# A two-pass graph layer with a gated feed-forward layer: table scatters spread over more groups, and four steps moved at the opening of both passes

## The reference, cut to what matters

```python
# x [50000, 256]; src, dst [50000]; 50000 edges
x = x + gnn(layernorm(x)); x = x + ffn(layernorm(x))
gnn(x) = x @ W1.T + b1 + (segment_sum(x[dst], src) / max(count, 1)) @ W2.T + b2
ffn(x) = shared_mlp(x) + sum over the top 2 of 4 experts of gate * expert_mlp(x)
```

## Time and profile before

| | us |
|---|---|
| median of 3 runs | 3266.72 (3265.14 to 3267.07) |
| profiled execution | 3267.08 |
| its span, from first to last instruction | 3265.5 |
| busy PE, DVE, ACT, POOL | 3104.3, 2673.0, 1944.1, 1831.9 |

### The profile page before, as it was taken

One profiled execution on the slowest core, in us unless ns is written; L12 is line 12 of the kernel. 1 busy time (PEld: TensorE's weight loads), 2 busy tenths in 40 slices (PEclk: granted clock), 3 DMA queues, 4 the chain that ended last, 5 costly groups with the idle time before them and its releaser, 6 DMA issues.

```text
span 3265.5 us, 61478 instructions
## 1 busy us (share of the span) xinstructions
PE 3104.3 (95%) x20817; PEld 2846.7 (87%) x20817; DVE 2673.0 (82%) x7212; ACT 1944.1 (60%) x3507; POOL 1831.9 (56%) x1554
## 2 busy tenths in 40 slices
PE   6988889989949999999999999999999999999998
PEld 6988888889948888888888888888888888888987
DVE  7878878786438888888888888888888888888886
ACT  4655555555626656566665656666665656666565
POOL 1688888888445554555555555555555555555540
PEclk9998899999979999999999999999999999999999
DMA  8776666676643333333333333333333333333330
GB/s 247 205 186 180 178 195 180 177 198 179 180 126 89 97 93 89 98 84 99 85 100 92 91 97 84 97 83 101 90 94 98 85 98 84 99 87 97 93 82 26
DMA packets 201856, 387.38 MB, mean 119 GB/s; under 512 B 106703, under 2 KB 109853, under 8 KB 201538
## 3 DMA queue, kind: packets, MB, share of 16 engines
q1 hardware_dynamic: 133938, 226.03, 25.6%
q10 hardware_dynamic: 30800, 102.42, 9.8%
q0 software_dynamic: 36800, 54.95, 7.2%
HBM read 236.11 MB, written 161.00 MB: 122 GB/s over the span
## 4 chain that ended last, share of the span: by engine, by line
PE 70%; DVE 0%; ACT 0%; DMA 0%; POOL 0%; issue 0%; SPq 0%; POOLq 0%; DVEq 0%
PE acc L1129 25%; PE acc L1190 13%; PE acc L1099 12%; PE acc L1110 4%; PE acc L1112 4%; PE acc L1176 3%; PE acc L1153 3%; PE acc L1186 1%; PE acc L1145 1%; PE acc L1201 1%; PE acc L1139 1%; DMA tab<-tab_d 0%; POOL e_oh L178 0%; POOL rows L166 0%; ACT h2f L1234 0%
## 5 line engine op out<-in xcount | busy, mean ns | idle before, releaser
L166 POOL DMA_INDIRECT rows<-z_d,tab x500 | 568.1, 1136 | 645.2 <-DMA tab<-tab_d 486.0
L178 POOL TENSOR_SCALAR e_oh<-iota_sb,tab 128x250 fp32r<-128x250 f32 (+1 forms) x500 | 522.6, 1056 | 470.2 <-PE acc L1112 466.5
L1129 PE MATMUL acc<-x1T_hi,wl_hl 128*128 128x500 f32 x2400 | 665.4, 392 | 0.0
L387 POOL DMA_INDIRECT tab_d<-pair,idx x400 | 555.0, 1387 | 118.9 <-issue 104.7
L726 PE MATMUL acc<-w_hl,xT_hi 128*125 128x256 f32 x3200 | 586.6, 289 | 0.0
L1129 PEld LDWEIGHTS acc<-x1T_hi,wl_hl 128*128 128x128 f32 x2400 | 444.0, 188 | 84.0
L726 PEld LDWEIGHTS acc<-w_hl,xT_hi 128*125 128x125 f32 x3200 | 483.2, 195 | 0.0
L1190 PE MATMUL acc<-wl_hl,h_hi 128*125 128x256 f32 x2400 | 477.7, 281 | 0.0
L1391 DVE TENSOR_TENSOR h_lo<-h1f,h_hi 128x500 fp32r<-128x500 f32 x600 | 396.8, 674 | 49.1 <-ACT h_hi L1228 39.7
L1221 ACT ACTIVATE h1f<-acc,bl_sb 128x500 f32<-128x500 f32 x600 | 404.2, 674 | 14.4
L1190 PEld LDWEIGHTS acc<-wl_hl,h_hi 128*125 128x125 f32 x2400 | 390.6, 185 | 3.7
(11 more groups left out here) (145 smaller groups left out, 6400.8 us busy)
## 6 DMA issues: line engine op xcount, KB each, us to landing
xs<-in_x SPq DMA_DIRECT2D x100, 448.0 KB
z_d<-zs ACTq DMA_DIRECT2D x100, 448.0 KB
y_d<-ys ACTq DMA_DIRECT2D x100, 448.0 KB
y_sb<-y_d SPq DMA_DIRECT2D x100, 448.0 KB
x_sb<-in_x SPq DMA_DIRECT2D x100, 448.0 KB
out<-x_sb SPq DMA_DIRECT2D x100, 448.0 KB
codes_b<-code_d SPq DMA_DIRECT2D x25, 390.6 KB
rows<-z_d,tab POOLq DMA_INDIRECT x500
```

Of the source, the lines that this page charges most:

```text
L166: pool.indirect_dma_start(out=rows[g.h][:, q, :], out_offset=None, in_=z_d, in_offset=bass.IndirectOffsetOnAxis(ap=tab[g.h][:, q, 0:1], ax ...
L178: pool.tensor_scalar(e_oh[:, q, w], iota_sb[:, w], tab[g.h][:, q, 1:2].bitcast(F32), None, ALU.is_equal).then_inc(S["e_oh_ready"], 1)
L387: pool.indirect_dma_start(out=tab_d, out_offset=bass.IndirectOffsetOnAxis(ap=idx[:, n:n + 1], axis=0), in_=pair[:, 2 * n:2 * n + ROW], in_ ...
L1129: mm = pe.matmul(bank[L1_BANKS[t]][:, 0:GN], wl1_hl[:, w, f, t * P:(t + 1) * P], (x1T_hi, x1T_lo)[a][:, f, :], start=n == 0, stop=n == 5)
```

## The change

The 400 scatters are spread over groups 8 to 96 with 9 for two groups, where 5 a group were done by group 87; three come before the power of an even group instead of two. The low bias row goes to partition 32 and is written there by DVE; `two_ones` is all ones (the other rows of `bias_r` are zero). SP's head loses the fills, which are issued two a group for groups 0 to 4, and the weights and constants of the main pass, which follow at groups 20 and 24; targets come before the identity. DVE takes the statistics and negative bias of groups 0 and 1 earlier, PE the edge transposes before group 0's. In the main pass, at step -2 alone, POOL's gathers come after the power.

```diff
@@ -57,7 +57,6 @@
 OB = 4
 G_WTS = 84
 NSC = 8
-PER_G = 5
 WINDOW = ((0, 2), (0, 2), (0, NS), (2, NS), (2, NS))
 
 
@@ -206,7 +205,6 @@
                 st_b = sb("st_b", [1, 2, D], F32, c0)
                 st_bs = sb("st_bs", [1, D], F32, c0)
                 st_bh = sb("st_bh", [1, D], F32R, c0)
-                st_bl = sb("st_bl", [1, D], F32R, c0)
                 b3_hi = sb("b3_hi", [NB3, D], F32R, c0)
                 b3_lo = sb("b3_lo", [NB3, D], F32, c0)
 
@@ -252,7 +250,6 @@
                 s_flo = sem("ffn_weights_low")
                 s_small = sem("small_weight_step")
                 s_bs = sem("bias_ready")
-                s_row = sem("bias_row_moved")
                 s_fillset = sem("fill_set")
                 s_filled = sem("table_filled")
                 s_one = sem("ones_ready")
@@ -313,14 +310,14 @@
                               .then_inc(s_bc[m % 2], 16)
 
                         sp.dma_start(ei[:, 0], src).then_inc(s_src, 16)
-                        sp.dma_start(code2[:], codes).then_inc(s_c2, 16)
                         load_x(0)
                         load_x(1)
                         sp.dma_start(st_w12[:, :, 0:D], w1t).then_inc(s_w12, 16)
                         sp.dma_start(st_w12[:, :, D:2 * D], w2t).then_inc(s_w12, 16)
                         sp.dma_start(st_b[:], b12.partition_broadcast(1)).then_inc(s_w12, 16)
+                        sp.dma_start(ei[:, 1], dst).then_inc(s_dst, 16)
                         sp.dma_start(ident_sb[:], ident).then_inc(s_id, 16)
-                        sp.dma_start(ei[:, 1], dst).then_inc(s_dst, 16)
+                        sp.dma_start(code2[:], codes).then_inc(s_c2, 16)
                         load_x(2)
                         load_x(3)
                         sp.wait_ge(s_code, 1)
@@ -330,27 +327,29 @@
                         sp.wait_ge(s_codest, 16)
                         load_codes(0)
                         load_codes(1)
-                        sp.wait_ge(s_fillset, 3)
-                        for k in range(NFILL):
-                            sp.dma_start(fill_v[0][:, k * FILL:(k + 1) * FILL], fill[:])\
-                              .then_inc(s_filled, 16)
-                        sp.wait_ge(s_bs, 7)
-                        sp.dma_start(bias_r[1:2].bitcast(F32), st_bl[:].bitcast(F32)).then_inc(s_row, 16)
-                        sp.dma_start(st_wl1[:], wl1).then_inc(s_wl, 16)
-                        sp.dma_start(st_wl2[:], wl2).then_inc(s_wl, 16)
-                        sp.dma_start(st_wl3[:], wl3).then_inc(s_wl, 16)
-                        sp.dma_start(st_gw[:], gw).then_inc(s_wl, 16)
-                        sp.dma_start(st_b3[:], b3).then_inc(s_wl, 16)
-                        sp.dma_start(st_sel[:], selg).then_inc(s_wl, 16)
-                        sp.dma_start(iota_sb[:], iota).then_inc(s_cst, 16)
-                        sp.dma_start(bl1_sb[:], bl1).then_inc(s_cst, 16)
-                        sp.dma_start(bl2_sb[:], bl2).then_inc(s_cst, 16)
-                        sp.dma_start(gb_sb[:], gb.partition_broadcast(P)).then_inc(s_cst, 16)
-                        sp.dma_start(tie_sb[:], tie).then_inc(s_cst, 16)
                         blocks = 2
                         for g in range(NG):
                             if g + XB < NG:
                                 load_x(g + XB)
+                            if g == 0:
+                                sp.wait_ge(s_fillset, 3)
+                            if 2 * g < NFILL:
+                                for k in (2 * g, 2 * g + 1):
+                                    sp.dma_start(fill_v[0][:, k * FILL:(k + 1) * FILL], fill[:])\
+                                      .then_inc(s_filled, 16)
+                            if g == 20:
+                                sp.dma_start(st_wl1[:], wl1).then_inc(s_wl, 16)
+                                sp.dma_start(st_wl2[:], wl2).then_inc(s_wl, 16)
+                                sp.dma_start(st_wl3[:], wl3).then_inc(s_wl, 16)
+                            if g == 24:
+                                sp.dma_start(st_gw[:], gw).then_inc(s_wl, 16)
+                                sp.dma_start(st_b3[:], b3).then_inc(s_wl, 16)
+                                sp.dma_start(st_sel[:], selg).then_inc(s_wl, 16)
+                                sp.dma_start(iota_sb[:], iota).then_inc(s_cst, 16)
+                                sp.dma_start(bl1_sb[:], bl1).then_inc(s_cst, 16)
+                                sp.dma_start(bl2_sb[:], bl2).then_inc(s_cst, 16)
+                                sp.dma_start(gb_sb[:], gb.partition_broadcast(P)).then_inc(s_cst, 16)
+                                sp.dma_start(tie_sb[:], tie).then_inc(s_cst, 16)
                             if blocks < NCH // CB4 and CB4 * (blocks - 1) <= last_chunk(g) + 1:
                                 load_codes(blocks)
                                 blocks += 1
@@ -394,13 +393,14 @@
                         rstd(1)
                         for g in range(NG):
                             if g >= G_SCAT:
-                                n = (g - G_SCAT) * PER_G
-                                for e in range(n, min(n + 2, EC)):
+                                n = min(EC, (g - G_SCAT) * 9 // 2)
+                                m = min(EC, (g + 1 - G_SCAT) * 9 // 2)
+                                for e in range(n, min(n + 3, m)):
                                     scatter(e)
                             if g % 2 == 0 and g + 4 < NG:
                                 rstd(g // 2 + 2)
                             if g >= G_SCAT:
-                                for e in range(n + 2, min(n + PER_G, EC)):
+                                for e in range(n + 3, m):
                                     scatter(e)
                         for h in range(NSC):
                             pool.wait_ge(s_scat[h], 16 * (EC // NSC))
@@ -546,7 +546,7 @@
                         dve.memset(ones16[:], 1.0).then_inc(s_one, 1)
                         dve.memset(zeros16[:], 0.0).then_inc(s_one, 1)
                         dve.memset(bias_r[:].bitcast(F32), 0.0).then_inc(s_bs, 1)
-                        dve.memset(two_ones[:].bitcast(F32), 0.0).then_inc(s_bs, 1)
+                        dve.memset(two_ones[:].bitcast(F32), 1.0).then_inc(s_bs, 1)
                         dve.memset(half_neg[:], -0.5).then_inc(s_bs, 1)
                         dve.memset(fill[:], 0).then_inc(s_fillset, 1)
                         dve.memset(pair[:], 0).then_inc(s_fillset, 1)
@@ -567,6 +567,7 @@
                         dve.wait_ge(s_half, 1)
                         dve.scalar_tensor_tensor(out=code16[:], in0=c_g, scalar=2.0, in1=c_h,
                                                  op0=ALU.mult, op1=ALU.add).then_inc(s_code, 1)
+                        stats(0)
                         dve.wait_ge(s_dst, 16)
                         dve.tensor_copy(flat[:, 0], ei[:, 1]).then_inc(s_flat, 1)
                         step(dve.tensor_scalar(c_t, c_s[:], float(SP_), 1.0, ALU.mult, ALU.add))
@@ -575,22 +576,19 @@
                         dve.scalar_tensor_tensor(out=flat[:, 2], in0=c_h, scalar=float(HALF),
                                                  in1=c_l, op0=ALU.mult,
                                                  op1=ALU.add).then_inc(s_flat, 1)
+                        neg_bias(0)
                         dve.wait_ge(s_w12, 16 * 3)
                         dve.tensor_tensor(st_bs[:], st_b[:, 0], st_b[:, 1], ALU.add).then_inc(s_bs, 1)
                         dve.wait_ge(s_bs, 4)
-                        dve.memset(two_ones[0:2].bitcast(F32), 1.0).then_inc(s_bs, 1)
                         dve.tensor_copy(st_bh[:], st_bs[:]).then_inc(s_bs, 1)
-                        dve.wait_ge(s_bs, 6)
-                        dve.tensor_tensor(st_bl[:], st_bs[:], st_bh[:].bitcast(F32),
+                        dve.wait_ge(s_bs, 5)
+                        dve.tensor_tensor(bias_r[32:33], st_bs[:], st_bh[:].bitcast(F32),
                                           ALU.subtract).then_inc(s_bs, 1)
                         dve.tensor_copy(bias_r[0:1], st_bh[:].bitcast(F32)).then_inc(s_bs, 1)
                         dve.wait_ge(s_whi, 1)
                         dve.tensor_tensor(w12_hl[:, 1], st_w12[:], w12_hl[:, 0].bitcast(F32),
                                           ALU.subtract).then_inc(s_wlo, 1)
-                        stats(0)
-                        neg_bias(0)
                         stats(1)
-                        neg_bias(1)
                         low(0)
                         for a in range(2):
                             dve.wait_ge(s_tr, a + 1)
@@ -600,6 +598,7 @@
                                 dve.tensor_copy(to[:, :, :, 0], got).then_inc(s_ev, 1)
                             else:
                                 dve.tensor_copy(to[:, :, :, 1].bitcast(F32), got).then_inc(s_ev, 1)
+                        neg_bias(1)
                         dve.wait_ge(s_c2, 16)
 
```

(9 more changed lines are left out.)

## The result

The changed kernel takes 3191.14 us (median of four runs, 3189.53 to 3193.37) against 3266.89 us (3265.14 to 3270.93) for the kernel before beside it: 75.8 us less, a ratio of 0.9767, 95% interval 0.975 to 0.9784. Forecast were 3189 us and 3179 to 3211. The profiled execution took 3193.37 us, with a span of 3191.8.

What follows compares the result with a forecast made beforehand. POOL's five scatters per group, with powers queued among them, were taken to limit the middle stage, PE the main pass. Gains of 55.8 + 13.1 + 10.0 less 1.0 made 77.9 us off 3267.1: 3189 us, range 3179 to 3211.

Steps and rivals of the forecast that it cites:

- What bounds the middle, and the spread: Middle stage: POOL's scatters and powers set the pace; 9 scatters per pair instead of 10 gain 55.8 us.
- rival 1: Middle stage: scatters cost more beside a denser VectorE, 8 us, or 15 if the delay doubles; chance 0.18.
- The margin at the end: End of first pass: last scatters, tables and one-hots stay hidden before the gather, with 6 us to spare.
- the last ten follow the last power: 15 us: End of first pass: ten scatters at 1.49 us after the last power, against 27.4 us of PE work.
- The start: First groups: PE's transposes of group 1 start at 22.9 instead of 36.06 us, gaining 13.1 us.
- I put 1 us for it: Early groups: cost of moving ten fills among groups 0 to 4, 1 us, bounds 0 and 12.
- Rival 2: Early groups: fills crowd out x loads and stores, giving the start back, 12 us, 3201 us; chance 0.08.
- The opening: Main pass's first rounds: power of group 0 ahead of gathers gains 10.0 us, bounds 5 and 11.
- 947.3 + 6.6 + 6.8 + 6.1: Opening's next round on POOL: gathers 2 and 3 and one-hots in sequence, power to 968.2, about 0.9 us late.
- Rival 3: Middle stage: another limit, such as a power-to-variance loop through VectorE; gain 43 us less, 3232 us; chance 0.07.
- Rival 4: PE's clock: slow stretches after more idle gaps make the kernel slower, granted clock about 0.8; chance 0.02.
- Rival 5: Middle stage: scatter count doesn't set the pace, groups stay at 9.36 us, 3266 us; chance 0.02.

Runs made afterwards that it cites:

- The start alone: The kernel before with bias row by VectorE, reordered heads, and fills and weights among the groups; scatters and opening as before: 3254.95 us, 13.5 us less.
- the thin fills: The changed kernel with one fill for each of groups 0 to 5 and two for groups 6 and 7: 3191.86 us.
- the earlier first scatter: The changed kernel with scatters from group 7 on, at 40 for 9 groups: 3184.9 us.
- the fills ahead: The changed kernel with all ten fills issued ahead of the group loop: 3196.73 us; unchanged copy beside it 3196.95.

## Why the prediction was right

It was right in the total by 2 us, and by its steps thus:

**What bounds the middle, and the spread.** Right. 725.35 us from power to power against 725.0. The sum against the tail: 26.7 us from the last power to PE's end (27.4 said), so the stretch gained 56.1 us against 55.8. The spread alone gave 52.6. That the sum hit 725.35 to half a microsecond is luck: four more profiles of kernels with the same middle took 720.66, 724.31, 726.44 and 727.73.

**The price of a scatter, rival 1.** Not seen at its size. The mean went from 1.406 to 1.413 us, where that rival needed 20 ns more at least; the fixed delay was the right reading, and its place is VectorE's counting, mostly its product, as the earlier trace rows hinted. The Trainium skill, SBUF — State Buffer (who interferes with whom), says that a VectorE instruction with two SBUF inputs contends with a GpSimd instruction that reads SBUF. The powers agree with it: 2.28 us beside a product and 1.68 otherwise. The same section of the Trainium skill has it that such a product doesn't hold back descriptor writing, marked as inferred. Here scatters beside it take 1.91 in place of 1.23 us, so for them the measurement decides against that sentence, unless it is their reading of indices that waits, which no run here separates.

**The margin at the end.** Wrong, though it changed nothing in this kernel. I wrote 6 us to spare; the gather waited 1.37. The step "the last ten follow the last power: 15 us" left out the power's own 1.69, and "some 2 us for the last scatter's landing" was too short: from the last scatter's end at 840.14 it was 4.8 us to the issue of the table's load, then 3.6 to its landing. The kernel with 35 scatters for eight groups has no such wait left (0.17 us) and pays for it: its earlier end of PE brings the gather no sooner.

**The start.** Mechanism right, 13.9 us at group 1 against 13.1. What failed is the term for the fills, "I put 1 us for it": by the power of group 12 4.3 us were gone (2.0 to 5.0 in six profiles with two fills a group). It was costed through the sum of bandwidth and by SP's queue; the cost came through ACT, whose store issue took 4.67 us. Rival 2 had the stores right, at a third of its size. The start alone lost 2.0 us by then and still gave 13.5 in total, so in the total the term isn't shown to be wrong.

**The opening.** Right: from first gather to the transposes of group 1 9.4 us less, against 10.0. The transposes of group 0 gained 12.1 of them (forecast 10.9), and 2.8 were given back by the next one (forecast 0.9). The prediction's own terms for that next power, 947.3 + 6.6 + 6.8 + 6.1, give 966.8 for its start and not 968.2 for its end; nothing else hangs on it. The power alone gave 11.8.

**Rival 3**, another limit in the middle, was absent there; one came up in the last groups, in a loop that I hadn't named: ACT between PE and PE. **Rival 4** went the other way, the granted clock in the middle rose from 0.91 to 0.97 with fewer idle gaps. **Rival 5** is excluded by the spread alone.

The terms as measured in the profiles: 56.1 + 9.5 + 9.4 = 75.0 us, and 1.4 lost between the transposes of the main pass's last group and the end, for which no step stood: 73.6, the difference of the spans within rounding, against 77.9. That the median came so near owes something to the 2 us by which the profiled execution lies above it.

## What to carry to other kernels

Where one engine does small equal tasks between the steps that others wait for, its pace is the count times the price plus issue time, and spreading them evenly gives back the engine's share, until the total of these tasks becomes the length of the stage; then their number, price or start matters. Parts in different stages added up here within what the runs can tell, so they can be forecast and tried alone. Parts that meet at the same wait, as the thin fills and the earlier first scatter did, need a look at what that wait ends on. A bulk transfer moved into a busy loop is to be costed at every engine that issues DMAs there, not only at the queue that carries it.

## What the runs showed of the hardware

- A scatter or a power on POOL beside VectorE's 16-bit product of two SBUF operands takes 0.5 to 0.8 us longer on average in the profiles above, about the 0.72 us of the two products; twice the products don't make twice the delay, and another form of the product moves it from scatters to powers. Some scatters are as long beside the running count alone.
- ACT's issue of two stores of y took 2.6 to 4.7 us near 40 us where two fills a group were being issued on another queue, 2.2 to 2.5 with thinner fills, under 1.6 with the fills ahead. That the fills' transfers hold the issue up is inferred from these three cases.
- The changed kernel differed by 5.8 us between two groups of runs, the kernel before by 1.4. That a kernel whose limits lie close together shows such differences more is a guess from this one case; the 7 us gained by starting from group 7 are shown on one chip only.
